# Window attention block: products with the values and sums of the probabilities on four column strips of the array instead of three

## What is computed

```python
y = layernorm(x) * norm1_w + norm1_b                      # over the 96 channels
q, k, v = split(y @ qkv_w.T + qkv_b)                      # 6 heads of 16, windows of 64 tokens
attn = softmax(q * 16**-0.5 @ k.T + mask)                 # 64 x 64 for each window and head
x = x + (attn @ v) @ proj_w.T + proj_b
x = x + gelu(layernorm2(x) @ mlp_w1.T + mlp_b1) @ mlp_w2.T + mlp_b2
out = x * rsqrt((x * x) @ gamma_eff.T + beta_eff)
```

## Time and profile before

| | |
|---|---|
| median of 3 runs | 1959.5 us (1957.79 to 1961.05) |
| profiled execution | 1959.52 us |
| its span, first to last instruction | 1957.6 us |
| TensorE busy | 1899.8 us, 97% |
| VectorE busy | 1690.2 us, 86% |
| ScalarE busy | 1640.4 us, 84% |
| GpSimd busy | 1642.1 us, 84% |

### The profile page before, as it was taken

How to read it: one execution, slowest core, us unless ns; L and a number is a source line. 1 busy time by engine, 2 the same in 40 slices (tenths; PEclk the granted TensorE clock), 3 DMA queues, 4 the chain that set the end, 5 groups by cost and what they waited for, 6 DMA issues and landing times.

```text
span 1957.6 us, 70164 instructions
## 1 busy us (share of the span) xinstructions
PE 1899.8 (97%) x26628; PEld 1335.6 (68%) x26628; DVE 1690.2 (86%) x4516; ACT 1640.4 (84%) x2945; POOL 1642.1 (84%) x1801
## 2 busy tenths in 40 slices
PE   4999999999999999999999999999999999999995
PEld 2676776776776766767677677667677677677663
DVE  5889988988889888988998898888898898898873
ACT  2788888888888888888888888888888888888884
POOL 4688888888888888888888888888888888888874
PEclk9999999999999999999999999999999999999997
DMA  3122222222122122122122122122122122122110
GB/s 61 28 41 49 38 47 49 35 50 49 35 50 49 34 51 49 34 51 50 32 54 50 31 53 49 32 52 48 35 52 46 36 52 45 38 51 46 28 30 24
DMA packets 217314, 85.00 MB, mean 43 GB/s; under 512 B 117286, under 2 KB 215912, under 8 KB 216984
## 3 DMA queue, kind: packets, MB, share of 16 engines
q1 hardware_dynamic: 216262, 80.22, 21.2%
q0 software_dynamic: 128, 0.20, 0.1%
q10 hardware_dynamic: 594, 0.12, 0.0%
HBM read 28.03 MB, written 25.17 MB: 27 GB/s over the span
## 4 chain that ended last, share of the span: by engine, by line
PE 95%; DVE 1%; issue 1%; ACT 1%; DMA 1%; SPq 1%; POOL 0%; POOLq 0%; DVEq 0%; ACTq 0%
PE mm_bank L900 48%; PE score_banks L956 10%; PE probs_t_bank L967 9%; PE pv_bank L981 6%; PE mm_bank L991 6%; PE turn_bank L893 6%; PE mm_bank L934 5%; PE turn_bank L886 4%; SPq L351 0%; DMA k_block<-k 0%; DMA x_ext<-in_x 0%; DVE y_tok L750 0%; DVE x L808 0%; PE score_banks L900 0%; DVE o_ext L815 0%
## 5 line engine op out<-in xcount | busy, mean ns | idle before, releaser
L438 POOL TENSOR_TENSOR hidden_lo<-hidden,hidden_hi 128x512 fp32r<-128x512 f32 x382 | 484.7, 1282 | 0.2 <-POOL hidden_hi L433 0.2
L779 DVE TENSOR_REDUCE row_max<-score_banks 128x12 f32<-128x768 f32 x256 | 243.7, 952 | 124.0 <-PE score_banks L956 124.0
L520 ACT ACT_TABLE_LOAD x256 | 328.4, 1283 | 4.5
L750 DVE TENSOR_SCALAR y_tok<-turn_bank,moments,rstd 128x96 f32<-128x96 f32 x1024 | 303.6, 369 | 5.7 <-ACT rstd L531 5.6
L566 ACT ACTIVATE probs_t<-probs_t_bank 128x384 f32<-128x384 f32 x512 | 249.7, 488 | 56.5 <-PE probs_t_bank L967 52.7
L587 ACT ACTIVATE hidden<-mm_bank 128x512 f32<-128x512 f32 x381 | 228.0, 598 | 62.8 <-PE mm_bank L900 47.8
L967 PE MATMUL probs_t_bank<-ident_sb,probs 128*128 128x128 f32 x1536 | 259.0, 277 | 1.9 <-ACT probs_t L566 1.8
L967 PEld LDWEIGHTS probs_t_bank<-ident_sb,probs 128*128 128x128 f32 x1536 | 189.0, 140 | 97.0 <-issue 36.8
L787 DVE TENSOR_TENSOR shifted<-score_banks,row_max 128x768 f32<-128x768 f32 x256 | 245.2, 958 | 8.4
L560 ACT ACTIVATE probs<-shifted 128x768 f32<-128x768 f32 x256 | 215.0, 840 | 27.4 <-DVE shifted L787 26.8
L433 POOL TENSOR_SCALAR hidden_hi<-hidden 128x512 fp32r<-128x512 f32 x382 | 231.3, 617 | 2.1 <-ACT hidden L587 2.1
(11 more groups left out here) (132 smaller groups left out, 4601.1 us busy)
## 6 DMA issues: line engine op xcount, KB each, us to landing
x_ext<-in_x SPq DMA_DIRECT2D x128, 192.0 KB, 3.3
k_block<-k SPq DMA_DIRECT2D x768, 32.0 KB, 2.1
out<-o_ext SPq DMA_DIRECT2D x128, 192.0 KB, 2.7
mask_stage<-in_qmask SPq DMA_DIRECT2D x64, 32.0 KB
y_hi<-mask_stage SPq DMA_DIRECT2D x64, 32.0 KB
k_block<-in_kmask POOLq DMA_DIRECT2D x2, 96.0 KB, 4.6
w_raw<-in_w_t SPq DMA_DIRECT2D x1, 144.0 KB
w<-in_w_t SPq DMA_DIRECT2D x1, 144.0 KB
```

The source lines that it names most:

```text
L438: nc.gpsimd.tensor_tensor(lo, whole, hi, ALU.subtract).then_inc(is_split, 1)
L520: nc.scalar.preload_act_table_set(name)
L750: made = nc.vector.tensor_scalar(y_tok[ln][:, c, :], turn_banks[ln][:, n * DIM:(n + 1) * DIM], moments[ln][:, c, 0:1], rstd[ln][:, c:c + 1 ...
L779: nc.vector.tensor_reduce(row_max[:, g, :, :], group_scores(), op=ALU.max, axis=AX.X)\
```

## The change

`times_v` and `sum_probs` use a fourth strip, columns 96 to 127, for the last pair of windows (the last 128 queries of the half). The other three pairs (`MAIN`, 384 columns) stay on strips 0 to 2. The matmuls of the values stay 24, now in 6 turns of four strips where there were 8 turns of three. The sums become six matmuls: three of 384 columns, and three of 128 columns in the fourth strip, where the three head pairs of the last window pair stand side by side. `log_sum` and `inv_sum` become 128 x 384. `divide` becomes four instructions: three of 32 x 128 bring the last pair's products from partitions 96 to 127 back to their head pair's rows of `attended`, then one of 96 x 384 does the rest and signals.

```diff
--- before.py
+++ after.py
@@ -42,6 +42,9 @@
 GROUP_PAIRS = PAIRS // GROUPS
 GROUP = GROUP_PAIRS * HEADS * TOKENS
 CHUNKS = HALF // 128
+STRIPS = HEAD_PAIRS + 1
+LAST = PAIRS - 1
+MAIN = LAST * 2 * TOKENS
 MASK_ROWS = 8
 LN_EPS = 1e-5
 PEDESTAL = 2.0 ** -36
@@ -124,8 +127,8 @@
         shifted = sb("shifted", [128, GROUPS, GROUP_PAIRS * TILE_HEADS, ROW_TILES, TOKENS])
         probs = sb("probs", [128, GROUPS, GROUP_PAIRS, TILE_HEADS, ROW_TILES, TOKENS])
         probs_t = sb("probs_t", [128, 2, HEAD_PAIRS, PAIRS, 128])
-        log_sum = sb("log_sum", [DIM, HALF])
-        inv_sum = sb("inv_sum", [DIM, HALF])
+        log_sum = sb("log_sum", [128, MAIN])
+        inv_sum = sb("inv_sum", [128, MAIN])
         attended = sb("attended", [DIM, HALF])
         attended_hi = sb("attended_hi", [DIM + 1, HALF], f32r)
         attended_lo = sb("attended_lo", [DIM + 1, HALF], f32r)
@@ -570,7 +573,7 @@
 
             def log_sums(A, a):
                 act.wait_ge(sums_made, A + 1)
-                nc.scalar.activation(log_sum[:, :], mm_bank("sum", a)[0:DIM, :], ACT.Ln)\
+                nc.scalar.activation(log_sum[:, :], mm_bank("sum", a)[:, 0:MAIN], ACT.Ln)\
                     .then_inc(log_sum_made, 1)
 
             def inverse_sums(A, a):
@@ -792,8 +795,12 @@
             def divide(A, a):
                 dve.wait_ge(inv_sum_ready, A + 1)
                 dve.wait_ge(pv_made, A + 1)
-                nc.vector.tensor_tensor(attended[:, :], pv_bank[0:DIM, :],
-                                        inv_sum[:, :], ALU.mult).then_inc(attended_ready, 1)
+                for m in range(HEAD_PAIRS):
+                    cols = slice(m * 2 * TOKENS, (m + 1) * 2 * TOKENS)
+                    nc.vector.tensor_tensor(attended[32 * m:32 * m + 32, MAIN:HALF], pv_bank[DIM:128, cols],
+                                            inv_sum[DIM:128, cols], ALU.mult)
+                nc.vector.tensor_tensor(attended[:, 0:MAIN], pv_bank[0:DIM, 0:MAIN],
+                                        inv_sum[0:DIM, :], ALU.mult).then_inc(attended_ready, 1)
 
             def first_residual(A, a):
                 dve.wait_ge(proj_made, A + 1)
@@ -973,23 +980,27 @@
                 pe.wait_ge(v_ready, A + 1)
                 wait(pe, attended_ready, A)
                 pe.wait_ge(probs_t_ready, PAIRS * (A + 1))
-                for p in range(PAIRS):
-                    for n in range(2):
-                        w = (a % 2) * HALF_WINDOWS + 2 * p + n
-                        for m in range(HEAD_PAIRS):
-                            first = (2 * p + n) * TOKENS
-                            made = nc.tensor.matmul(pv_bank[32 * m:32 * m + 32, first:first + TOKENS],
-                                                    v_block[:, w, m, :],
-                                                    probs_t[:, a % 2, m, p, n * TOKENS:(n + 1) * TOKENS],
-                                                    start=True, stop=True)
+                for turn in range(2 * LAST):
+                    at, n = turn // 2, turn % 2
+                    first = turn * TOKENS
+                    for strip in range(STRIPS):
+                        m, p = (strip, at) if strip < HEAD_PAIRS else (at, LAST)
+                        made = nc.tensor.matmul(pv_bank[32 * strip:32 * strip + 32, first:first + TOKENS],
+                                                v_block[:, (a % 2) * HALF_WINDOWS + 2 * p + n, m, :],
+                                                probs_t[:, a % 2, m, p, n * TOKENS:(n + 1) * TOKENS],
+                                                start=True, stop=True)
                 made.then_inc(pv_made, 1)
 
             def sum_probs(A, a):
 
                 mm_wait("sum", A)
                 for m in range(HEAD_PAIRS):
-                    made = nc.tensor.matmul(mm_bank("sum", a)[32 * m:32 * m + 32, :], ones_pair_sb[:, :],
-                                            probs_t[:, a % 2, m, :, :], start=True, stop=True)
+                    nc.tensor.matmul(mm_bank("sum", a)[32 * m:32 * m + 32, 0:MAIN], ones_pair_sb[:, :],
+                                     probs_t[:, a % 2, m, 0:LAST, :], start=True, stop=True)
+                for m in range(HEAD_PAIRS):
+                    made = nc.tensor.matmul(mm_bank("sum", a)[DIM:128, m * 2 * TOKENS:(m + 1) * 2 * TOKENS],
+                                            ones_pair_sb[:, :], probs_t[:, a % 2, m, LAST, :],
+                                            start=True, stop=True)
                 made.then_inc(sums_made, 1)
 
             def project(A, a):
```

## The result

The changed kernel takes 2028.46 us (median of 4 runs, 2027.86 to 2033.74); the kernel before takes 1958.64 us beside it. The ratio is 1.0361, 95% interval 1.034 to 1.0381: slower. The forecast was 2026 us, in a range of 1990 to 2044. The profiled execution's span grew from 1957.6 to 2027.0 us.

What follows compares the result with a forecast made beforehand. TensorE was taken to bound, VectorE 0.26 us behind at L808. The division's +0.87 us less 0.26 gave 0.61 a round, 122 rounds +74, stalls -9, ends +2: 1959.5 + 67 = 2026 us, range 1990 to 2044.

Steps and rivals of the forecast that it cites:

- The bound: Each round: TensorE bounds, VectorE 0.26 us behind; the projection hangs on L808, so no round is shorter than 14.39 us.
- Values and sums: TensorE's first stretch: values 0.22 us less, sums 0.24 us less, with the fourth strip running beside the others.
- The 0.3 to 0.4 us that were to reach L808: TensorE's 0.46 us gain, less what is lost waiting for the denominators' bank, as it arrives at L808's wait.
- ScalarE: `log_sum` and `inv_sum` at 384 columns each lose some 0.13 us; costed at nothing, since the division's inputs are ready earlier.
- The division: On VectorE, four instructions in place of one take 1.46 us in place of 0.59: +0.87 us a round.
- all four lose the overlap: VectorE's divisions each change starting partition, so none starts before its predecessor ends; small ones 0.30 us apart; chance 0.74.
- The sum: Whole kernel: 122 rounds x 0.61 us = +74, stalls -9, ends +2, total +67 us.
- The term per round: Period grows from 14.65 to 15.26 us: 0.87 us more on VectorE less L808's 0.26 us wait, 0.61 us.
- The term of -9 us for stalls hidden in TensorE's new slack: Rounds where TensorE stalls: its 1.0 us to spare hides much of the 14 us; -9, bounds 0 and -14.
- the low value for the ends: At both ends, some 3 rounds without L808's 0.26 us wait pay 0.87 us in full: +2 us.
- The narrower range of 2012 to 2044: Own range of the all-held case, from 0.29 to 0.33 us a small division and the stalls' bounds.
- dearer: Each small division costs 0.36 us or more, or TensorE's longer wait costs clock: 2045 us and up; chance 0.04.

Runs made afterwards that it cites:

- Experiments 10 and 11: `y2` split moved behind the second residual, first residual ahead of the outputs, on VectorE: on the kernel before 1958.28 us, on the changed kernel 1962.26 us.
- experiment 4: Changed kernel, its three small divisions reading from partition 0 and writing a spare tile at partitions 0, 32 and 64: 2010.33 us.
- experiment 3: Changed kernel, its three small divisions all reading from partition 96 and writing a spare tile at partition 96: 2005.6 us.
- experiment 2: Changed kernel, its three small divisions all reading from partition 0 and writing a spare tile at partition 0: 1975.45 us.
- experiment 5: Kernel before, with one more 32x128 multiplication at partition 0 ahead of the division, result unused: 1970.73 us.
- experiment 8: Changed kernel with values on three strips and one 96x512 division as before; ScalarE moves the last pair's inverse sums in four exponentials: 1959.3 us.
- experiment 6: Kernel before, with three more 32x128 multiplications at partition 0 ahead of the division, results unused: 1992.62 us.

## Why the prediction was right

**The bound.** The prediction held that TensorE bounds with VectorE 0.26 us behind, and that the loop closes through L808 and the projection. That was so. Experiments 10 and 11 show it from both sides: with TensorE as the bound, an earlier place for L808 gives nothing (1958.3 us); with VectorE as the bound, it gives 66 us, and TensorE's idle time before the projection falls by the 0.60 us of the `y2` split.

**Values and sums.** Four strips cost what three cost per column: 0.67 us for the values (0.68 forecast). The sums' fourth strip runs beside the others: its first three instructions start at 1007.55, between the two sets of L998 at 1007.52 and 1007.85. The forecast of 0.73 us for the sums can't be read off, since the denominators wait for their bank. The 0.3 to 0.4 us that were to reach L808 were 0.41; the argument had 0.30 at the denominators (0.31 measured), and not the 0.09 that the keys win because the logarithm ends in time. Without the small divisions the strips are worth 45 us (46 forecast).

**ScalarE.** Costed at nothing, rightly for this kernel: the 0.09 us at the keys only lengthen TensorE's wait before the projection, and VectorE's division comes after the inverse sums here as before (they end at 1010.05 + 0.51 = 1010.56, it starts at 1011.58). Its two instructions take 0.49 and 0.51 us.

**The division.** The steps were: first small one 0.10 us later than with overlap, each 0.30 to its successor, the large one 0.46. Measured: 1011.58 - 1011.18 = 0.40 where 0.29 was usual, 0.11 more; 0.31; 0.48. The sum is 0.11 + 0.92 + 0.48 - 0.59 = +0.92 us, against +0.87. The choice that made the forecast, that all four lose the overlap, is seen in the rows of the changed kernel, and experiments 2 to 4 show that it comes from the move. Whether input and output count each by itself was open when the forecast was made: the copies change both together, and that all four lose the overlap was the author's estimate. The traces show that either change was enough: the input's at the first small division of the changed kernel, the output's in experiment 4. In experiment 3 the first and the large division lack the overlap: they start 0.40 and 0.30 us after their predecessor, the two between them 0.22 and 0.21. In experiment 4 the second, the third and the large one lack it (0.28, 0.30 and 0.29 us), while the first has it (0.29 us after the last normalisation, as the one division before). In experiment 2 all have it: 0.28 and three times 0.20 us.

**The sum.** The term per round was 0.61 us; it is 15.29 - 14.65 = 0.64. The number of rounds was put at 122, of which 119 can be counted, so that the two small errors partly cancel (74 us forecast, 76 measured). Over 119 rounds it can be read off the second residual's starts, here of the changed kernel and then of the kernel before:

```profile
96.88 0.74 DVE L815 SCALAR_TENSOR_TENSOR x<-mm_bank,b_col,x 96x512 f32<-96x512 f32 x1
...
1918.52 0.74 DVE L815 SCALAR_TENSOR_TENSOR x<-mm_bank,b_col,x 96x512 f32<-96x512 f32 x1
```

```profile
1849.45 0.75 DVE L808 SCALAR_TENSOR_TENSOR x<-mm_bank,b_col,x 96x512 f32<-96x512 f32 x1 [0.18 <-PE mm_bank L900]
```

With 94.48 us as the second kernel's start, the change is 1821.64 - 1754.97 = 66.7 us, of the 69.4 us by which the span grew. 119 x 0.64 = 76 us would be the undisturbed part. The kernel before spent 1754.97 - 119 x 14.65 = 12 us on TensorE's stalls, the changed one 1821.64 - 119 x 15.29 = 2. The term of -9 us for stalls hidden in TensorE's new slack was right at about -10; the slightly small term per round and the low value for the ends make up the 2.5 us by which the forecast was short. The narrower range of 2012 to 2044 does not follow from its own terms: 0.29 us a small one with stalls of -14 gives 2018, 0.33 with no relief 2047. The measured time lies in either. Of the rival "dearer", the part on the clock did not happen either: the mean granted clock was 0.995 in the changed kernel's profile and 0.993 in that of before.

**What the argument had not priced.** The second way from VectorE to TensorE, through the outputs and the first residual, was 0.1 us from deciding (0.14 us from the first residual's end to the transposes before, 0.05 where TensorE waits). So VectorE had 0.26 us to spare at L808 only, and not in the round. It didn't matter for the changed kernel, where the outputs mostly take 0.68 us, but it sank the expectation of experiment 5. And the expectation of experiment 8 had no term for when the four exponentials end, although the division waits for them.

## What to carry to other kernels

When one engine shows 97% busy, look for the wait that the second engine still has in each round: here it was 0.26 us, and what three more multiplications added beyond that was paid (experiment 6). Look for a second such place too: one more multiplication of 0.20 us fitted into the first wait and still cost 12 us at another (experiment 5). The products moved to spare partitions had to be brought back here as PSUM was emptied, and there several small VectorE instructions that change their starting partition cost about half as much again as ones that stay (0.29 to 0.31 us against 0.20). If such work is needed, put it where the chain doesn't pass, or take other work out of the chain: a new order, with the `y2` split behind the second residual, gave back 66 of the 70 us.

## What the runs showed of the hardware beyond that

**VectorE and GpSimd held each other up.** The outputs' multiplication, with two inputs in SBUF, took 1.61 us in the kernel before while GpSimd's subtraction ran. In the changed kernel, where it starts first, it takes 0.68, and GpSimd's takes 1.80 in place of 1.29. The kernel before, GpSimd and VectorE:

```profile
1010.21 1.29 POOL L438 TENSOR_TENSOR y_lo<-y,y_hi 96x512 fp32r<-96x512 f32 x1 [0.18 <-POOL y_hi L433]
```

```profile
1010.43 1.61 DVE L815 TENSOR_TENSOR o_ext<-x,inv_den 96x512 f32<-96x512 f32 x1
```

The changed kernel:

```profile
1016.11 1.80 POOL L441 TENSOR_TENSOR y_lo<-y,y_hi 96x512 fp32r<-96x512 f32 x1 [0.18 <-POOL y_hi L436]
```

```profile
1016.08 0.68 DVE L822 TENSOR_TENSOR o_ext<-x,inv_den 96x512 f32<-96x512 f32 x1
```

In each pair the one that started first ran at its usual length (1.29 us for GpSimd's subtraction, 0.68 us for the multiplication) and the other one took longer; in the changed kernel 0.03 us lay between the starts. In the kernel before GpSimd's ended at 1010.21 + 1.29 = 1011.50 and VectorE's at 1010.43 + 1.61 = 1012.04, 0.54 us later, somewhat less than the 0.68 us that the multiplication takes where it starts first. That the multiplication starts first there is also why VectorE is busy only 17 us more in the changed kernel: in the groups by form the divisions grow from 86.8 to 112.9 + 70.9 = 183.8 us, while the outputs fall from 186.3 to 93.8. What makes the later instruction take longer the runs don't show.

**ScalarE's small exponentials don't overlap either.** The three of 128 columns, which change their starting partition, take 0.94 us together, 0.31 each (experiment 8), while the next ordinary instruction there starts 0.10 us before its predecessor's end (1004.00 against 1004.10). That the move is the reason is not shown: no run has small exponentials that stay where they are.

**Matmuls of different strips did not start in program order.** All of L998's instructions stand ahead of L1001's in the program. Three of them start from 1007.52 and three from 1007.85, while the first of L1001's start at 1007.55, ahead of the second three.
